# One run of all tiles with engine loops and copied row numbers, in a two-layer mixer and expert kernel

## The chip, the cores and the metric

The kernel runs on one core of a Trainium2 chip. Its time is the device time of one execution in microseconds (us). Five engines work side by side, each through its own list of instructions: TensorE (PE), VectorE (DVE), ScalarE (ACT), GpSimd (POOL) and SyncE (SP, which here only starts transfers). They meet at semaphores. PEld is TensorE's loading of weights, which runs beside its matmuls.

## The reference, cut to what matters

Two images of 128 channels and 64 by 64 positions pass two layers. Each layer has a mixer and then an expert network (eight experts, each token goes to two of them).

```python
x = x + _L0_conv_ref(_ln_c(x), ...)       # layer 0: one gate for each image and channel
t = _to_tokens(x)                          # 2 x 4096 tokens of 128 channels
t = t + _L0_ffn_ref(_ln_t(t), ...)         # softmax over 8 experts, best 2, shares normalised
x = _from_tokens(t, x)
x = x + _L1_conv_ref(_ln_c(x), ...)        # max pools of sizes 1 to 13, two of them blended by a score
t = _to_tokens(x)
t = t + _L1_ffn_ref(_ln_t(t), ...)         # experts with exact gelu, best 2
x = _from_tokens(t, x)
# one expert:  y = gelu(x @ W1 + b1) @ W2 + b2, 128 -> 512 -> 128
```

## The kernel before

**Units and tiles.** A unit is one layer for one image: unit 0 and 1 are layer 0 for image 0 and 1, unit 2 and 3 are layer 1. For each unit the 8192 pairs of token and expert are sorted by expert and cut into 39 tiles of 256 slots. Tiles are counted 0 to 155 through the program; 39, 78 and 117 are the first of units 1, 2 and 3. Step j of a unit is one turn of the loop in `tile_steps`.

**One tile** passes these stages. POOL gathers its rows of tokens with two indirect DMAs of 128 rows (`gather`, L450: `xg<-xn_rows`). PE transposes them (`turn_x`, L697) and ACT copies the result (`copy_x`, L520: `xT`). PE makes the hidden values (`up`, L706), ACT applies gelu (`activate`, L531: `hT`), PE multiplies by the second matrix (`down`, L718), ACT copies (`copy_y`, L541), PE transposes back (`turn_y`, L728), ACT copies (`copy_rows`, L550: `yr`), and POOL scatters the rows with two more indirect DMAs (`scatter`, L459: `y_rows<-yr`). SP loads the weights of the tile's expert (`load_weights`, L351), three tiles ahead. xg, the weights and yr are rings of four buffers (`RING`).

**The order in a step** is fixed in the code: for step t, PE does `turn_x` of tile t+1, `up` of t, `down` of t-1, `turn_y` of t-2; ACT copies in the same order; POOL gathers tile t+4 (`G_AHEAD`) and then scatters tile t-2. An engine takes its list in order, so what waits holds back everything behind it.

**Runs.** `RUNS = [(0,), (1,), (2,), (3,)]`: each unit is a run of its own. It ends with two more steps that empty the pipeline, and the next unit's first gathers follow the last scatter on POOL. All steps are written out; no engine loops.

**Work between the tiles.** `WHEN` lists for each unit at which step (and fraction: after `up`, after `down`) every engine puts in the work for other units. In unit 0 that is the routing of unit 1. In unit 1 it is, for image 0: `outputs` (SP waits for all scatters of unit 0, then loads its results, L368), `combine` on DVE (L1146, which adds the experts' results to the tokens), `mix_state` and `mix_norm` (PE turns tokens to channels, ACT copies), the max pools on DVE (L1177 to L1196), and then the routing of unit 2: `route_turn` (L644 on PE, L503 on ACT), `route_products` (L661), DVE's choice of experts (L1025 on), `route_slots` (L671), four `route_invert` of 16 matmuls (L681), after which DVE has the row numbers (L1112 to L1120). Unit 2 does the same for image 1 and the routing of unit 3. DVE takes this in the order of the program, without regard to steps. In unit 3 only results are combined, and the final turning back of image 0 stands at step 20.

**Row numbers.** DVE writes them for a whole unit into `tile_rows`, and the indirect DMAs read the column of their tile from there.

## Time and profile before

| | |
|---|---|
| median of 3 runs | 1268.28 us (1260.07 to 1268.85) |
| the profiled execution | 1272.95 us |
| its span, first to last instruction | 1271.1 us |
| mean granted TensorE clock | 0.824 of full |
| busy: PE, DVE, ACT, POOL | 923.5, 579.4, 545.1, 706.6 us |
| first gather; first ACT copy of xT of units 0, 1, 2, 3 | 158.4; 165.9, 426.0, 709.3, 990.3 us |
| last ACT copy of a tile's rows; end | 1234.2; 1271.1 us |

Busy shares are averages over stages with different limits; indirect DMAs on POOL count as busy while POOL writes their descriptors. A row of the timeline gives start, length, engine, line, operation, what it writes and reads, the count, and in brackets how long the engine had been idle before it and what it waited for. Ends of matmuls are modelled, so the times at which ACT starts a copy are the surer mark of when PE was done. "remote" in a wait means that the profile has no record of what released it in time.

### The profile page before, as it was taken

What the parts mean: (1) busy time and instruction counts of PE and PEld (TensorE: products, weight loads), DVE (VectorE), ACT (ScalarE), POOL (GpSimd) and SP (SyncE); (2) the same over time, 40 slices, a digit from 0 to 9 for tenths busy, and PEclk for the clock granted to TensorE, in tenths of its full rate; (3) what the DMA queues carried; (4) which work ended last, traced back from release to release, by engine and by line L of the source; (5) the groups of instructions that cost most, each with busy time, mean ns of one, the idle gap of its engine ahead of it and who ended that gap; (6) DMA issues with size and microseconds to landing.
All of it is one profiled execution on the core that took longest, in us unless ns stands there. A gap on an engine that the chain in (4) does not pass through costs nothing.

```text
span 1271.1 us, 14305 instructions
## 1 busy us (share of the span) xinstructions
PE 923.5 (73%) x4116; PEld 740.2 (58%) x4116; DVE 579.4 (46%) x1273; ACT 545.1 (43%) x1363; POOL 706.6 (56%) x650
## 2 busy tenths in 40 slices
PE   5216568899977579765998679776988677778772
PEld 4115256776765468554866567665866556666551
DVE  7977822270300647995470738995460003100006
ACT  6303144462444356443553455443553334545341
POOL 3410065576665657787353657887254567656662
PEclk8555578998998789998888789988788789878895
DMA  3000323353544634433162634443153246435435
GB/s 143 1 0 17 116 87 106 101 160 101 188 137 116 216 114 144 127 122 112 56 164 91 218 118 139 132 129 97 58 165 106 78 149 205 157 100 194 112 83 199
DMA packets 51453, 154.32 MB, mean 121 GB/s; under 512 B 14432, under 2 KB 14453, under 8 KB 50864
## 3 DMA queue, kind: packets, MB, share of 16 engines
q1 hardware_dynamic: 31408, 116.11, 27.0%
q0 software_dynamic: 19968, 37.29, 10.9%
q8 instruction: 35, 0.57, 0.2%
q14 instruction: 42, 0.34, 0.1%
HBM read 123.96 MB, written 33.03 MB: 124 GB/s over the span
## 4 chain that ended last, share of the span: by engine, by line
PE 40%; issue 15%; another core or an unknown queue 12%; POOL 12%; ACT 10%; DVE 6%; DMA 5%; POOLq 0%; ACTq 0%; DVEq 0%; SPq 0%
PE h_ps L706 14%; PE yT_ps L718 11%; POOL y_rows L459 6%; POOL xg L450 6%; PE acc_ps L681 6%; PE turn_ps L644 4%; DMA xg<-xn_rows,tile_rows 4%; ACT hT L531 4%; PE acc_ps L661 2%; PE xT_ps L697 2%; PE yr_ps L728 1%; ACT work L568 1%; ACT yr L550 1%; DVE tok L1146 1%
## 5 line engine op out<-in xcount | busy, mean ns | idle before, releaser
L459 POOL DMA_INDIRECT y_rows<-yr,tile_rows x312 | 337.4, 1081 | 316.4 <-ACT yr L550 230.2
L450 POOL DMA_INDIRECT xg<-xn_rows,tile_rows x312 | 330.9, 1060 | 186.1 <-issue 93.9
L706 PE MATMUL h_ps<-xT,expert 128*128 128x256 f32 x1248 | 354.8, 432 | 57.0 <-ACT hT L531 46.4
L718 PE MATMUL yT_ps<-hT,expert 128*128 128x256 f32 x1248 | 326.8, 409 | 23.3 <-ACT yT L541 14.2
L531 ACT ACTIVATE hT<-h_ps,expert 128x256 f32<-128x256 f32 x624 | 255.3, 477 | 154.2 <-PE h_ps L706 79.9
L706 PEld LDWEIGHTS h_ps<-xT,expert 128*128 128x128 f32 x1248 | 257.2, 218 | 106.5 <-issue 52.2
L718 PEld LDWEIGHTS yT_ps<-hT,expert 128*128 128x128 f32 x1248 | 257.3, 209 | 73.7 <-ACT yT L541 19.4
L1146 DVE SCALAR_TENSOR_TENSOR tok<-work,share,tok 128x128 f32<-128x128 f32 x224 | 66.0, 368 | 379.4 <-DMA work<-y_rows 287.5
L541 ACT ACTIVATE yT<-yT_ps,expert 128x256 f32<-128x256 f32 x156 | 74.3, 476 | 192.1 <-PE yT_ps L718 112.4
L697 PE MATMUL xT_ps<-ident,xg 128*128 128x128 f32 x312 | 69.0, 306 | 113.0 <-DMA xg<-xn_rows,tile_rows 105.7
L520 ACT ACTIVATE xT<-xT_ps 128x256 f32<-128x256 f32 x156 | 60.5, 388 | 188.3 <-PE xT_ps L697 114.9
L697 PEld LDWEIGHTS xT_ps<-ident,xg 128*128 128x128 f32 x312 | 40.6, 155 | 128.7 <-DMA xg<-xn_rows,tile_rows 116.1
L644 PE MATMUL turn_ps<-ident,tok 128*128 128x128 f32 x192 | 38.5, 358 | 52.2 <-DVE tok L1142 25.2
L896 DVE BATCH_NORM_STATS2 stats<-tok 128x6 f32<-128x128 f32 x192 | 39.4, 288 | 78.7 <-ACT tok L503 46.1
L550 ACT ACTIVATE yr<-yr_ps 128x256 f32<-128x256 f32 x156 | 59.5, 382 | 34.1 <-PE yr_ps L728 24.8
L1196 DVE SCALAR_TENSOR_TENSOR state<-work,mix_hot,state 128x1344 f32<-128x1344 f32 (+1 forms) x42 | 66.4, 1637 | 0.5
L644 PEld LDWEIGHTS turn_ps<-ident,tok 128*128 128x128 f32 x192 | 29.6, 184 | 59.7 <-DVE tok L1142 27.0
L728 PE MATMUL yr_ps<-ident,yT 128*128 128x128 f32 x312 | 62.0, 282 | 2.8 <-ACT yr L550 2.8
L728 PEld LDWEIGHTS yr_ps<-ident,yT 128*128 128x128 f32 x312 | 45.3, 147 | 19.8 <-ACT yT L541 3.7
L644 PE MATMUL turn_ps<-ident,state 128*128 128x128 f32 x192 | 34.1, 330 | 26.6 <-ACT tok L503 9.7
L1183 DVE TENSOR_TENSOR work<-work 128x1344 f32<-128x1344 f32 (+1 forms) x36 | 53.1, 1532 | 0.4
L1177 DVE TENSOR_TENSOR work<-work 128x1302 f32<-128x1302 f32 (+1 forms) x36 | 53.1, 1531 | 0.3
(187 smaller groups left out, 730.3 us busy)
## 6 DMA issues: line engine op xcount, KB each, us to landing
expert<-in_experts SPq DMA_DIRECT2D x156, 514.5 KB
work<-y_rows SPq DMA_DIRECT2D x32, 512.0 KB, 6.8
xn_rows<-work SPq DMA_DIRECT2D x16, 512.0 KB, 3.8
xg<-xn_rows,tile_rows POOLq DMA_INDIRECT x312
y_rows<-yr,tile_rows POOLq DMA_INDIRECT x312
state<-in_x SPq DMA_DIRECT2D x4, 1024.0 KB, 8.1
out<-state SPq DMA_DIRECT2D x8, 512.0 KB
shared<-in_first SPq DMA_DIRECT2D x1, 323.5 KB
```

The source lines that it names most:

```text
L450: pool.indirect_dma_start(xg[:, s, h, :], None, xn_rows[unit], bass.IndirectOffsetOnAxis(ap=tile_rows[unit % 2][:, at, 0, h:h + 1], axis=0)) \
L459: pool.indirect_dma_start(y_rows[unit], bass.IndirectOffsetOnAxis(ap=tile_rows[unit % 2][:, at, 1, h:h + 1], axis=0), yr[:, s, h, :], None ...
L531: ins = act.activation(hT[:, s, c, :], h_ps[c // 2][:, c % 2, :], func, bias=expert[:, t.slot(RING), BIAS + c:BIAS + c + 1])
L541: act.activation(yT[:, s, :], yT_ps[:, 0:SLOTS], ACT.Identity, bias=expert[:, t.slot(RING, d), EXPERT - 1:EXPERT]) \
L550: act.activation(yr[:, s, :, :], yr_ps[:, 0:HALVES, :], ACT.Copy).then_inc(s_yr_sb, 1)
L644: mm = pe.transpose(bank[:, k * P:(k + 1) * P], source(t), ident[:])
L681: mm = pe.matmul(acc_ps[:, 0:2 * n], hot_lane[:, :, t], hot_block[:, :, :, t] .rearrange("p a q -> p (a q)"), start=(k == 0 and t == 0), s ...
L697: mm = pe.transpose(xT_ps[:, h * P:(h + 1) * P], xg[:, t.slot(RING, d), h, :], ident[:])
L706: mm = pe.matmul(h_ps[c // 2][:, c % 2, :], expert[:, t.slot(RING), c * P:(c + 1) * P], xT[:, t.slot(2), :], start=True, stop=True)
L718: mm = pe.matmul(yT_ps[:, 0:SLOTS], expert[:, t.slot(RING, d), HIDDEN + c * P:HIDDEN + (c + 1) * P], hT[:, s, c, :], start=(c == 0), stop= ...
L728: mm = pe.transpose(yr_ps[:, h, :], yT[:, s, h * P:(h + 1) * P], ident[:])
L1146: ins = dve.scalar_tensor_tensor(tok[b][:, t, :], work_tok[1 + k][:, t, :], share[b][:, k, t:t + 1], tok[b][:, t, :], ALU.mult, ALU.add)
```

## The change

All units become one run (`RUNS = [(0, 1, 2, 3)]`): no emptying between them, the tile loop of PE, ACT, POOL and SP goes on across a unit's border. Near a border the gathers look ahead by 2 tiles (`BORDER`) instead of 4, worked out by `reach` and `due`. On POOL the scatter of tile t-2 now stands ahead of the gathers of a step.

From step 7 (`PEEL`) on, wherever at least 8 steps follow without work in between, an engine runs them in a loop of 4 tiles (`Fori`) with semaphore values in registers. [...] `tile_rows` becomes float, since ACT converts.

The mixing and routing steps stand at other places: fewer fractions, more in one place.

```diff
-RUNS = [(0,), (1,), (2,), (3,)]
+RUNS = [(0, 1, 2, 3)]
+BORDER = 2
 ...
-    return [(0, "outputs", b, 0, 1, 2, 3), (2, "mix_state", b, 0), (3, "mix_state", b, 1), (4, "mix_state", b, 2),
+    return [(1, "outputs", b, 0, 1, 2, 3), (4, "mix_state", b, 0), (5, "mix_state", b, 1), (6, "mix_state", b, 2),
 ...
+def reach(s, ahead, short):
+    unit, j = divmod(s, TILES)
+    last = (unit + 1) * TILES - 1
+    first = next(r for r in RUNS if unit in r)[0] * TILES
+    end = next(r for r in RUNS if unit in r)[-1] * TILES + TILES - 1
+    if s < first or (j == 0 and s > first):
+        return s + (ahead if s < first else short)
+    return min(end, s + ahead if s + ahead <= last else max(last, s + short))
 ...
 def tile_steps(eng, unit, step, between):
 ...
+    while j < TILES + 2 * ends_run(unit):
+        if j < TILES:
+            insert(j)
+        end = min([int(p) for p in between if p > j] + [TILES - AHEAD])
+        if j >= PEEL and end - j >= 2 * RING:
+            times = (end - j) // RING
+            with eng.Fori(0, times) as i:
+                for k in range(RING):
+                    step(Tile(unit, j + k, i), lambda part: None)
 ...
             def gather(t, d):
-                if t.old(d - RING):
-                    pool.wait_ge(s_xt_ps, t.done(d - RING))
+                pool.wait_ge(s_g_idx, t.done(d))
+                pool.sem_inc(s_begun, 1)
                 for h in range(HALVES):
-                    ...IndirectOffsetOnAxis(ap=tile_rows[unit % 2][:, at, 0, h:h + 1], axis=0))
+                    ...IndirectOffsetOnAxis(ap=g_slot[:, s, h:h + 1], axis=0))
 ...
                 def step(t, mid):
-                    if t.has(G_AHEAD):
-                        gather(t, G_AHEAD)
                     if t.has(-2):
                         scatter(t, -2)
+                    for d in due(t, G_AHEAD, BORDER):
+                        gather(t, d)
 ...
+            def set_gather(t, d):          # on ACT
+                unit, at = t.at(d)
+                act.activation(g_slot[:, t.slot(RING, d), :], tile_rows[unit % 2][:, bass.ds(at, 1), 0, :]
+                               .rearrange("p a h -> p (a h)"), ACT.Copy).then_inc(s_g_idx, 1)
 ...
             def copy_rows(t, d):
+                act.activation(s_slot[:, s, :], tile_rows[unit % 2][:, bass.ds(at, 1), 1, :]
+                               .rearrange("p a h -> p (a h)"), ACT.Copy)
```

The other places are: mixing `mix_state` 4 to 7 (were 2 to 5), `mix_norm` 9.3 in one piece (7.3 to 8.3), `mix_score` 10 and 11 (9 and 10.3), `route_turn` and `route_products` 30 in one piece (27.6 to 28.6), `route_slots` 31 (31.3), `route_invert` 33 and 34 (33.3 to 35.3); in unit 0 `route_turn` 9 (4 and 6), products 10 and 11 (8 and 10), slots 14 (13.3), `route_invert` 20 and 21 (20 to 24).

**POOL at the border from unit 0 to unit 1**, before. L450 is a gather, L459 a scatter, two DMAs for a tile; the first row is the end of unit 0's steps.

```order
L450 DMA xg<-xn_rows,tile_rows 128x128 x2
L459 DMA y_rows<-yr,tile_rows 8192x128 x14
L450 DMA xg<-xn_rows,tile_rows 128x128 x14
L459 DMA y_rows<-yr,tile_rows 8192x128 x2
L450 DMA xg<-xn_rows,tile_rows 128x128 x2
```

The same place with the change (L500 gather, L509 scatter).

```order
L500 DMA xg<-xn_rows,g_slot 128x128 x2
L509 DMA y_rows<-yr,s_slot 8192x128 x6
L500 DMA xg<-xn_rows,g_slot 128x128 x2
L509 DMA y_rows<-yr,s_slot 8192x128 x2
L500 DMA xg<-xn_rows,g_slot 128x128 x2
L509 DMA y_rows<-yr,s_slot 8192x128 x2
L500 DMA xg<-xn_rows,g_slot 128x128 x2
L509 DMA y_rows<-yr,s_slot 8192x128 x2
L500 DMA xg<-xn_rows,g_slot 128x128 x6
L509 DMA y_rows<-yr,s_slot 8192x128 x2
```

Before, all seven last scatters pass and then seven tiles are gathered in a row. Now three scatters (tiles 33, 34, 35) pass and tile 39 is gathered; then scatter 36 and gather 40, scatter 37 and gather 41, scatter 38 and gathers 42, 43 and 44.

**PE at the routing of unit 2**, in unit 1, before, from the first half of `route_turn` (steps 27 to 31).

```order
L644 MATMUL turn_ps<-ident,state 128x128 x16
L697 MATMUL xT_ps<-ident,xg 128x128 x2
L706 MATMUL h_ps<-xT,expert 128x256 x4
L661 MATMUL acc_ps<-routerT,state 128x8 x16
L718 MATMUL yT_ps<-hT,expert 128x256 x4
L661 MATMUL acc_ps<-routerT,state 128x8 x16
L728 MATMUL yr_ps<-ident,yT 128x128 x2
```

The same with the change, from step 30.

```order
L713 MATMUL turn_ps<-ident,state 128x128 x32
L730 MATMUL acc_ps<-routerT,state 128x8 x32
L766 MATMUL xT_ps<-ident,xg 128x128 x2
L775 MATMUL h_ps<-xT,expert 128x256 x4
L787 MATMUL yT_ps<-hT,expert 128x256 x4
L797 MATMUL yr_ps<-ident,yT 128x128 x2
L740 MATMUL turn_ps<-chosen_any,before 128x256
L740 MATMUL turn_ps<-chosen_any,ones 128x256
```

The routing is packed together and begins two to three steps later; the four pieces of 16 inverting matmuls become two of 32.

## Rows read from the trace of the kernel before

**Rows 1.** Who waited for whom: us in total, times, longest.

```profile
POOL y_rows L459 <- ACT yr L550: 230.2, 62, 18.3
...
ACT hT L531 <- remote: 56.9, 32, 4.8
```

**Rows 2.** Windows, copies of xT on ACT alone: us, busy (count), clock, DMA share, GB/s.

```profile
294.20:400.00 105.80, 6.58 (x17) 0.90 0.45 137
...
510.00:586.00 76.00, 4.60 (x12) 0.95 0.41 127
...
1010.00:1105.00 95.00, 5.82 (x16) 0.89 0.51 167
```

**Rows 3.** Windows, POOL alone, while DVE makes the max pools.

```profile
510.50:586.00 75.50, 60.87 (x49) 0.95 0.41 128
```

**Rows 4.** Timeline, ACT in unit 3: two of its stops.

```profile
1004.34 0.84 ACT L531 ACTIVATE hT<-h_ps,expert 128x256 f32<-128x256 f32 x2 [4.75 <-remote]
...
1021.33 0.38 ACT L520 ACTIVATE xT<-xT_ps 128x256 f32<-128x256 f32 x1 [1.70 <-remote]
```

**Rows 5.** The page: the DMA queue that brings instructions, packets, MB, share.

```profile
q8 instruction: 35, 0.57, 0.2%
```

**Rows 6.** Timeline at the border to unit 1: ACT's copies of tiles 38, 39, 42, outputs, PE.

```profile
400.08 0.39 ACT L520 ACTIVATE xT<-xT_ps 128x256 f32<-128x256 f32 x1
...
414.96 0.98 POOL L459 DMA_INDIRECT y_rows<-yr,tile_rows  x1 [0.30 <-issue]
...
417.11 4.35 SPq L368 DMA_DIRECT2D work<-y_rows  x8
...
422.37 4.42 DVE L1146 SCALAR_TENSOR_TENSOR tok<-work,share,tok 128x128 f32<-128x128 f32 x16 [86.10 <-DMA work<-y_rows]
...
425.98 0.38 ACT L520 ACTIVATE xT<-xT_ps 128x256 f32<-128x256 f32 x1 [14.62 <-PE xT_ps L697]
...
427.94 3.62 PE L706 MATMUL h_ps<-xT,expert 128*128 128x256 f32 x8
...
431.77 1.89 PE L706 MATMUL h_ps<-xT,expert 128*128 128x256 f32 x8
...
436.83 0.39 ACT L520 ACTIVATE xT<-xT_ps 128x256 f32<-128x256 f32 x1
```

**Rows 7.** Timeline, ACT: one step at full clock.

```profile
969.57 0.39 ACT L520 ACTIVATE xT<-xT_ps 128x256 f32<-128x256 f32 x1
...
973.20 0.38 ACT L550 ACTIVATE yr<-yr_ps 128x256 f32<-128x256 f32 x1
```

**Rows 8.** Timeline: a copy of rows, its scatters, the next gather, all in unit 3.

```profile
1010.14 0.38 ACT L550 ACTIVATE yr<-yr_ps 128x256 f32<-128x256 f32 x1
...
1011.32 1.02 POOL L459 DMA_INDIRECT y_rows<-yr,tile_rows  x1 [8.34 <-ACT yr L550]
...
1013.95 0.99 POOL L450 DMA_INDIRECT xg<-xn_rows,tile_rows  x1 [0.30 <-issue]
```

**Rows 9.** Timeline: the first gather of unit 3, and ACT's copy of that tile.

```profile
985.74 0.99 POOL L450 DMA_INDIRECT xg<-xn_rows,tile_rows  x1 [0.30 <-issue]
...
990.25 0.38 ACT L520 ACTIVATE xT<-xT_ps 128x256 f32<-128x256 f32 x1 [9.41 <-PE xT_ps L697]
```

**Rows 10.** Timeline in unit 1: max pools begin, routing's turns begin, tile 77's copy.

```profile
482.29 0.16 DVE L1165 TENSOR_REDUCE gap<-gap_parts 128x1 f32<-128x8 f32 x1 [21.82 <-ACT work L510]
...
590.74 1.04 PE L644 MATMUL turn_ps<-ident,state 128*128 128x128 f32 x8
...
684.70 0.39 ACT L520 ACTIVATE xT<-xT_ps 128x256 f32<-128x256 f32 x1
```

**Rows 11.** Windows, the inverting matmuls L681 alone: PE and PEld busy (count).

```profile
590.00:678.30 88.30, 18.33 (x64) 9.42 (x64) 0.80 0.36 99
```

**Rows 12.** Lines, by form: small instructions near those that are added on ACT.

```profile
L531 ACT ACT_TABLE_LOAD x5 | 6.4, 1283 | 1.4 <-issue 1.4
...
L510 ACT ACTIVATION_READ_ACCUMULATOR work<-turn_ps 128x1 f32 x16 | 3.2, 202 | 0.0
```

More of the change, by code:

```diff
@@ L100, with __init__ @@
 class Tile:
-    def __init__(self, unit, j):
-        self.s = unit * TILES + j
+    def __init__(self, unit, j, i=None):
+        self.s, self.i = unit * TILES + j, i
         run = next(r for r in RUNS if unit in r)
         self.first, self.last = run[0] * TILES, (run[-1] + 1) * TILES - 1
+        self.loop_unit, self.loop_at = unit, j
     def at(self, d=0):
+        if self.i is not None:
+            return self.loop_unit, self.i * RING + (self.loop_at + d)
         return divmod(self.s + d, TILES)
     def has(self, d=0):
-        return self.first <= self.s + d <= self.last
+        return self.i is not None or self.first <= self.s + d <= self.last
     def old(self, d):
@@ L116, in done @@
     def done(self, d=0, per=1, part=None):
-        return (self.s + d) * per + (per if part is None else part)
+        n = (self.s + d) * per + (per if part is None else part)
+        return n if self.i is None else self.i * (RING * per) + n
     def slot(self, n, d=0):
@@ L122, in landed, with tile_steps @@
     def landed(self, d=0, each=1):
-        return ((self.s + d) // RING + 1) * 16 * each
-def tile_steps(unit, step, between):
-    extra = 2 * ends_run(unit)
+        n = ((self.s + d) // RING + 1) * 16 * each
+        return n if self.i is None else self.i * (16 * each) + n
+def tile_steps(eng, unit, step, between):
     def insert(at):
@@ L131, in insert, with due @@
             between[round(at, 1)]()
-    for j in range(TILES + extra):
-        insert(j)
-        step(Tile(unit, j), lambda part, j=j: insert(j + part))
-    if extra:
-        insert(TILES + extra)
+    j = 0
+    while j < TILES + 2 * ends_run(unit):
[7 more added lines that the diff above has]
+                    step(Tile(unit, j + k, i), lambda part: None)
+            j += times * RING
+        else:
+            step(Tile(unit, j), lambda part, j=j: insert(j + part))
+            j += 1
+    insert(TILES)
+def reach(s, ahead, short):
[6 more added lines that the diff above has]
+    return min(end, s + ahead if s + ahead <= last else max(last, s + short))
+def due(t, ahead, short):
+    if t.i is not None:
+        return [ahead]
+    if t.s > t.last:
+        return []
+    before = reach(t.s - 1, ahead, short) if t.s > t.first else t.first + ahead - 1
+    return [n - t.s for n in range(before + 1, reach(t.s, ahead, short) + 1)]
 def begins_run(u):
@@ L248, in build @@
         tile_expert = [sb(f"tile_expert{i}", [P, TILES], I32) for i in range(2)]
[L249 removed]
+        tile_rows = [sb(f"tile_rows{i}", [P, TILES, 2, HALVES]) for i in range(2)]
         gap_parts = sb("gap_parts", [P, GROUPS])
@@ L585, in tiles @@
                 if begins_run(u):
+                    act.wait_ge(s_rows, u + 1)
+                    for d in range(G_AHEAD):
+                        set_gather(Tile(u, 0), d)
                     copy_x(Tile(u, 0), 0)
+                    set_gather(Tile(u, 0), G_AHEAD)
                 def step(t, mid):
@@ L590, in step @@
                         copy_x(t, 1)
+                    ahead = due(t, AHEAD, BORDER + 1)
+                    if ahead == [AHEAD]:
+                        set_gather(t, AHEAD)
                     if t.has(0):
@@ L598, in step @@
                         copy_rows(t, -2)
-                tile_steps(u, step, plan(u, route_turn=route_turn, route_exp=route_exp, mix_state=mix_state, mix_norm=mix_norm,
+                    if ahead != [AHEAD]:
+                        for d in ahead:
+                            if t.at(d) == (u + 1, 0):
+                                act.wait_ge(s_rows, u + 2)
+                            set_gather(t, d)
+                tile_steps(act, u, step, plan(u, route_turn=route_turn, route_exp=route_exp, mix_state=mix_state, mix_norm=mix_norm,
                                               route_rows=route_rows, mix_score=mix_score, last_turn=last_turn))
```

58 lines of the change are left out of this document (31 added, 27 removed).

## The prediction, made before the result was known

> **What bounds the kernel now.** I read the page first, then who waited for whom, then windows over single stages, then the timeline at a border. The busy shares (PE 73%, POOL 56%) name no bound, so I went by pace: how often ACT copies an xT, once for each tile.
>
> The waits say that POOL's scatters stood 230.2 us for ACT's copies of rows [rows 1], so POOL is mostly not late. In the windows unit 0's second half makes 17 tiles in 105.8 us, 6.2 us a tile, and unit 3 has 16 copies, 15 intervals, in 95 us, 6.3 us a tile [rows 2]. Two floors lie below. PE's own step at full clock takes 3.63 us from ACT's xT to its yr [rows 7]. POOL's four DMAs take 5.2 us a tile: a pair of scatters 1013.95 - 1011.32 = 2.63 us [rows 8], and a pair of gathers about as much.
>
> While DVE makes the max pools, POOL is the bound: 49 DMAs busy for 60.87 us plus 0.30 us of issue each are 75.6 of 75.5 us [rows 3], and a tile takes 6.3 us [rows 2]. Outside it, something else costs 1 us a tile. ACT's timeline shows it: about 17 us apart, so every third tile, ACT stands on "remote" [rows 4], 56.9 us for hT alone [rows 1], although the gathers and weights of those tiles had landed before. PE must have been late there, with its list as the suspect: 35 packets of instructions, 0.57 MB, came through one queue [rows 5], and that is a third thing that comes at a steady count of PE instructions. I take these stops as the price of the written-out list, with less certainty than the two floors.
>
> **The change, part by part.** The sum is made against the profiled execution, 1272.95 us.
>
> *Borders.* Before, from ACT's copy of the last tile of unit 0 to that of the fourth of unit 1: 436.83 - 400.08 = 36.75 us [rows 6]; the other two borders are alike. What is removed is the emptying and the empty start. What is added is a new chain: POOL gathers tile 39 only after scatter 35, 40 after 36, 41 after 37, 42 after 38. Tile 35's rows are copied at the end of PE's step 37, and tile 39 is the first thing that PE wants in step 38; `up` of tile 38 is queued behind it on PE, and ACT, and so POOL's next scatter, wait behind that. The chain is: yr copy to scatter 1011.32 - 1010.14 = 1.18 us, two scatters 2.63 us [rows 8], first gather to ACT's copy of its tile 990.25 - 985.74 = 4.51 us [rows 9]: 8.32 us in which PE does nothing. Then the step, 3.63 us at full clock [rows 7]. Four such: 4 x 11.95 = 47.8 us. But PE idles for 8 us in each, and after an idle stretch it runs at the low level: behind the border of before, 8 matmul records took 3.62 us against 1.89 us one tile later [rows 6], 1.2 against 2.4 GHz. With the last three steps at that level it is 47.8 + 3 x 3.63 = 58.7 us. I take the middle, 53: +16 us a border, **+48 us** for three; bounds +33 and +66.
>
> *Outputs before weights.* SP waits at step 1 for the last scatter, then issues eight loads of 512 KB, then the weights of the fifth tile. Before, PE was not waiting then. From yr 38: 1.18 + 1.3 + 2.15 (last scatter to outputs, 417.11 - 414.96 [rows 6]) = 4.6 us, then 4.2 MB at the page's best slices, 200 GB/s, 21 us, so 26 us; PE wants these weights 8.3 + 3 x 5 = 23 us after yr 38. **+3 us** a kernel for one partial wait in three; 0 to +12.
>
> *The DVE chain.* Outputs of unit 0 come at about 400 + 12 + 28 + 5 + 5 = 450 instead of 417, so `combine` starts at 455 instead of 422.4 [rows 6], 33 us later. Does unit 2 wait for it? From `combine` to the normalised rows takes 482.29 - 21.82 - 422.37 = 38 us, and then DVE idled 21.8 us for PE and ACT [rows 10]. Now: rows at 493, `mix_norm` in one piece about 12 us, max pools from 506, 590.74 - 482.29 = 108 us long [rows 10], ready at 614. PE comes to step 30 after 20.7 steps of 5.7 us, at 624. So DVE's lateness is just swallowed by its old idle time and PE decides. From there 15.6 us of turns, 8 of products, 18.3 of inverting matmuls [rows 11], 7 steps of about 4.5, 8 us of waiting for the one-hots: 82 us to the copy of tile 77, at 706; before 684.70 [rows 10]. That is +21 us for a unit of which the border is 16 and the weights 1: **+8 us** for units 1 and 2 together beyond what is counted; -10 to +25, since the packed routing may save up to 12 us a unit and a late DVE cost as much.
>
> *Loops.* PE loops over 12 steps in unit 0, 16 each in units 1 and 2, 24 in unit 3. In units 1 and 2 they lie under the max pools, where POOL is the bound [rows 3]: nothing gained. In unit 0 and 3 the pace can fall from 6.2 to POOL's 5.2 plus 0.1 for register and semaphore instructions: 36 steps x 1.0 = -36 us. In unit 0 ACT's loop holds two table loads of 1.28 us [rows 12] in each of four turns, since an exp stands just ahead of it; half of 10 us is on the path: +5. Together **-30 us**; bounds 0 (the stops stay) and -45. The rule of the Trainium skill, Runtime: NRT & Kernel Launch, section Instruction fetch mechanics, speaks against this: fetching a straight list is said to be hidden, and a taken branch that leaves the loaded window to stall. By it, the loops would give nothing and the sum stood at +64; the stops in the trace, with inputs there, disagree with its first half, and of its second half no row shows anything.
>
> *The copies of row numbers* are 312 more instructions on ACT, nearest to the accumulator reads of 0.2 us [rows 12]: 0.4 us a tile on an engine that is 43% busy, beside PE. On the path lies one before the first gather. On POOL two increments and a few register instructions a tile count where it is saturated, some 40 tiles: 0.1 us each, **+5 us** in all; 0 to +12.
>
> *Packing of unit 0's routing:* the same PE work in larger pieces; POOL catches up after each. 0, -8 to +8.
>
> Sum: 48 + 3 + 8 - 30 + 5 = +34 us, 1272.95 + 34 = 1307 us. The median of the runs is 4.7 us below the profiled execution, so **1302 us**.
>
> **The rivals.**
>
> 1. *The loops give nothing back.* Each backward branch or each crossing inside the body (four tiles of PE's list) costs what the stops cost. For: the stops were not tied to a cause by any row. Against: a body that repeats need not be brought again. -30 becomes 0: 1332 us.
> 2. *Even.* PE recovers its clock inside each border step (+33 instead of +48), the weights are in time, the packed routing saves the 8 that I charge: 33 + 0 + 0 - 30 + 0 = +3, about 1270 us. For: the low level lasted one tile at the border shown [rows 6]. Against: here the idle stretch comes back each step.
> 3. *Faster: the stops are the real bound of the routing stretches.* The packed routing takes large matmul groups out of the tile steps; the path from `route_turn` to the last tile, 94 us now (590.74 to 684.70 [rows 10]), falls to its work, 15.6 + 8 + 18.3 + 7 x 3.63 = 67 us, in units 1 and 2, -27 each against my -12: -30 us more. It decides if the routing ends more than 20 us before step 37 wants its rows. Sum +4; with the loops at -45 and the borders at +33 it is -26, 1242 us. For: DVE idled there for PE. Against: DVE's own 13 us of one-hots stand between, and POOL still needs 5.2 us a step.
>
> Chances: my forecast 0.50, rival 1 0.15, even 0.20, faster 0.15. What a measurement here can tell from no change is about 1%, 12.7 us. So slower by over 1% 0.65, within 1% 0.20, faster 0.15. The range leaves out most of the faster case and the far tail of rival 1: 1262 to 1342 us; the forecast's own is 1285 to 1325.
>
> **What the next profile would show.** Right: at each border four intervals of 11 to 15 us between ACT's copies of xT, PE idle about 8 us in each with a gather as the releaser, and a low clock; `combine` of unit 1 some 30 us after the unit's first tile instead of before it; loops in unit 3 at 5.2 to 5.4 us a tile without "remote" waits; the max pool stretch still at 6.3. Wrong: border intervals under 10 us; `route_turn` waiting for DVE by more than 10 us; loop steps at 6 us or more, with instruction packets not much fewer than 35.

## The result, and the profile after

The changed kernel takes 1383.34 us (median; 1377.72 to 1388.62), the kernel before 1267.45 us: a ratio of 1.093, 95% interval 1.086 to 1.100, about 116 us slower. Forecast were 1302 us and a range of 1262 to 1342. The direction was right, the size was not.

The page of the changed kernel, profiled at 1377.72 us, has these lines (busy time and share; the clock by fortieths; the instruction queue; the chain; then groups with busy time, mean and what ended the idle time before them):

```profile
span 1375.9 us, 15949 instructions
...
PE 936.5 (68%) x4116; PEld 750.2 (55%) x4116; DVE 578.5 (42%) x1273; ACT 584.3 (42%) x1682; POOL 701.8 (51%) x650
...
PEclk8555599988888799998777699999878788899885
...
q8 instruction: 27, 0.44, 0.1%
...
PE 36%; issue 18%; DMA 11%; DVE 9%; POOL 9%; another core or an unknown queue 9%; ACT 7%; POOLq 0%; ACTq 0%; DVEq 0%; SPq 0%
...
L509 POOL DMA_INDIRECT y_rows<-yr,s_slot x312 | 336.1, 1077 | 426.8 <-ACT yr L607 341.7
...
L766 PE MATMUL xT_ps<-ident,xg 128*128 128x128 f32 x312 | 72.8, 320 | 245.1 <-DMA xg<-xn_rows,g_slot 221.9
```

The last group's line before:

```profile
L697 PE MATMUL xT_ps<-ident,xg 128*128 128x128 f32 x312 | 69.0, 306 | 113.0 <-DMA xg<-xn_rows,tile_rows 105.7
```

Work hardly grew (ACT by 39 us, its slot copies and table loads). Waiting did: POOL's scatters stood 341.7 us for ACT's copies of rows where they had stood 230.2 [rows 1], and PE stood 221.9 us for gathers where it had stood 105.7. The loops were there: 27 instruction packets in place of 35 [rows 5].

ACT's copies of xT give a clock with one tick a tile. Against before, the changed kernel was behind at tile 38 by 13.0 us, at tile 42 by 33.7, at 77 by 44.1, at 81 by 68.9, at 116 by 73.3, at 120 by 93.3 and at 155 by 100.4; the tail adds 4.4. Nearly two thirds of it (65.5 of 104.8 us) were lost in three times four tiles, 38 to 42, 77 to 81 and 116 to 120. The timeline of the second and third interval of the first border (start, duration, engine, line, operation; idle time and releaser in brackets):

```profile
438.36 0.69 PE L766 MATMUL xT_ps<-ident,xg 128*128 128x128 f32 x2 [7.97 <-DMA xg<-xn_rows,g_slot]
438.84 3.52 PE L775 MATMUL h_ps<-xT,expert 128*128 128x256 f32 x8
...
442.20 1.89 PE L787 MATMUL yT_ps<-hT,expert 128*128 128x256 f32 x8
...
444.59 0.37 ACT L607 ACTIVATE yr<-yr_ps 128x256 f32<-128x256 f32 x1
...
445.85 1.01 POOL L509 DMA_INDIRECT y_rows<-yr,s_slot  x1 [9.02 <-ACT yr L607]
447.16 1.00 POOL L509 DMA_INDIRECT y_rows<-yr,s_slot  x1 [0.30 <-issue]
448.47 0.99 POOL L500 DMA_INDIRECT xg<-xn_rows,g_slot  x1 [0.30 <-issue]
...
452.98 0.38 ACT L574 ACTIVATE xT<-xT_ps 128x256 f32<-128x256 f32 x1 [7.92 <-PE xT_ps L766]
```

From ACT's copy of rows to its next copy of xT are 452.98 - 444.59 = 8.39 us (forecast 8.32), in which PE does nothing. Then comes a step in two halves: the eight matmuls of `up` take 3.52 us, the eight of `down` 1.89 us. The granted clock was 0.50 in the first half and 1.00 in the second, so PE has its full clock back inside each step and goes idle with it. From xT to rows the step takes 5.50 us (439.09 to 444.59), between the 3.63 us of full clock [rows 7] and twice that. The windows of these two halves, and of the whole interval of tile 42 (busy PE, PEld, DVE, ACT, POOL, then the granted clock, DMA share, GB/s):

```profile
438.80:442.10 3.30, 3.30 (x10) 2.68 (x9) 0.00 (x0) 1.22 (x3) 0.00 (x0) 0.50 0.00 0
442.20:444.60 2.40, 2.11 (x11) 1.61 (x9) 0.00 (x0) 1.31 (x5) 0.00 (x0) 1.00 0.00 0
...
453.00:470.50 17.50, 5.77 (x21) 4.62 (x21) 0.92 (x4) 3.15 (x11) 7.75 (x8) 0.70 0.34 106
```

Over the three borders eight of the twelve gaps from rows to the next xT take 8.3 to 8.5 us, and eleven of the twelve steps 5.3 to 6.1 us (the very first 3.54). The last gap of each border is longer, at the first border so:

```profile
462.25 0.99 POOL L500 DMA_INDIRECT xg<-xn_rows,g_slot  x1 [0.30 <-issue]
463.09 4.91 SPq L417 DMA_DIRECT2D work<-y_rows  x8
...
469.81 0.69 PE L766 MATMUL xT_ps<-ident,xg 128*128 128x128 f32 x2 [11.73 <-DMA xg<-xn_rows,g_slot]
...
470.54 0.38 ACT L574 ACTIVATE xT<-xT_ps 128x256 f32<-128x256 f32 x1 [11.52 <-issue]
```

From this gather to ACT's copy of its tile are 8.29 us, where the three gathers before it took 4.5. The eight loads of unit 0's outputs (`work<-y_rows`) start beside it. At the second border, also with outputs, the same stretch is 8.7 us; at the third, where none are loaded, 5.7.

The DVE chain of unit 1: combine, the pools' begin, their last piece, the routing's turns:

```profile
469.58 17.39 DVE L1215 SCALAR_TENSOR_TENSOR tok<-work,share,tok 128x128 f32<-128x128 f32 x64 [145.14 <-DMA work<-y_rows]
...
524.08 0.16 DVE L1234 TENSOR_REDUCE gap<-gap_parts 128x1 f32<-128x8 f32 x1 [18.22 <-ACT work L558]
...
621.83 4.74 DVE L1265 SCALAR_TENSOR_TENSOR state<-work,mix_hot,state 128x1344 f32<-128x1344 f32 x3
...
645.12 1.04 PE L713 MATMUL turn_ps<-ident,state 128*128 128x128 f32 x8
```

ACT's copy of tile 77 follows at 728.8. DVE's result is there at 626.6, and the turns stand ahead of PE's step 30, at 645.1: 18.5 us unused. Before, DVE's last piece began at 581.02, and the turns ran at 590.74 [rows 10], 5 us after its end.

The stops that the prediction hoped to be rid of are still there inside the loops. ACT in unit 3:

```profile
1194.87 1.57 ACT L585 ACTIVATE hT<-h_ps,expert 128x256 f32<-128x256 f32 x4 [5.96 <-remote]
...
1273.04 0.84 ACT L585 ACTIVATE hT<-h_ps,expert 128x256 f32<-128x256 f32 x2 [4.45 <-remote]
```

Windows over 35 copies of xT in unit 3, before and then changed, give 214.9 and 219.5 us, 6.1 and 6.3 us a tile:

```profile
1010.30:1225.20 214.90, 13.33 (x35) 0.87 0.48 152
```
```profile
1106.10:1325.60 219.50, 13.40 (x35) 0.89 0.47 149
```

### The profile page after: what moved, and what is told of

Read it like the earlier page. It is cut to its first block, busy times and chain, and to the rows that moved or that the text cites. A ratio compares the mean times of both kernels' runs of the same rounds, so it can differ in the third digit from the quotient of the medians.

```text
span 1375.9 us, 15949 instructions
## 1 busy us (share of the span) xinstructions
PE 936.5 (68%) x4116; PEld 750.2 (55%) x4116; DVE 578.5 (42%) x1273; ACT 584.3 (42%) x1682; POOL 701.8 (51%) x650
## 4 chain that ended last, share of the span: by engine, by line
PE 36%; issue 18%; DMA 11%; DVE 9%; POOL 9%; another core or an unknown queue 9%; ACT 7%; POOLq 0%; ACTq 0%; DVEq 0%; SPq 0%
PE h_ps L775 13%; DMA xg<-xn_rows,g_slot 10%; PE yT_ps L787 8%; PE acc_ps L750 5%; POOL xg L500 5%; POOL y_rows L509 4%; PE turn_ps L713 4%; PE acc_ps L730 3%; ACT hT L585 3%; PE xT_ps L766 2%; ACT yr L607 1%; DVE tok L1215 1%; ACT yT L595 1%; DVE stats L965 1%
## 5 line engine op out<-in xcount | busy, mean ns | idle before, releaser
L509 POOL DMA_INDIRECT y_rows<-yr,s_slot x312 | 336.1, 1077 | 426.8 <-ACT yr L607 341.7
L500 POOL DMA_INDIRECT xg<-xn_rows,g_slot x312 | 327.0, 1048 | 185.5 <-issue 92.3
L775 PE MATMUL h_ps<-xT,expert 128*128 128x256 f32 x1248 | 374.7, 453 | 26.5 <-ACT hT L585 21.4
L787 PE MATMUL yT_ps<-hT,expert 128*128 128x256 f32 x1248 | 315.0, 398 | 10.5 <-ACT yT L595 7.6
L775 PEld LDWEIGHTS h_ps<-xT,expert 128*128 128x128 f32 x1248 | 272.9, 230 | 75.6 <-ACT hT L585 25.5
L787 PEld LDWEIGHTS yT_ps<-hT,expert 128*128 128x128 f32 x1248 | 253.8, 204 | 57.4 <-ACT yT L595 11.9
L766 PE MATMUL xT_ps<-ident,xg 128*128 128x128 f32 x312 | 72.8, 320 | 245.1 <-DMA xg<-xn_rows,g_slot 221.9
L713 PE MATMUL turn_ps<-ident,tok 128*128 128x128 f32 x192 | 34.9, 336 | 48.9 <-DVE tok L1211 25.3
L750 PE MATMUL acc_ps<-hot_blocks,shared 128*128 128x156 bf16 x128 | 36.6, 455 | 24.3 <-DVE hot_blocks L1162 21.8
```

The source lines that it names most:

```text
L500: pool.indirect_dma_start(xg[:, s, h, :], None, xn_rows[t.at(d)[0]], bass.IndirectOffsetOnAxis(ap=g_slot[:, s, h:h + 1], axis=0)) \
L509: pool.indirect_dma_start(y_rows[t.at(d)[0]], bass.IndirectOffsetOnAxis(ap=s_slot[:, s, h:h + 1], axis=0), yr[:, s, h, :], None, bounds_ch ...
L713: mm = pe.transpose(bank[:, k * P:(k + 1) * P], source(t), ident[:])
L750: mm = pe.matmul(acc_ps[:, 0:2 * n], hot_lane[:, :, t], hot_block[:, :, :, t] .rearrange("p a q -> p (a q)"), start=(k == 0 and t == 0), s ...
L766: mm = pe.transpose(xT_ps[:, h * P:(h + 1) * P], xg[:, t.slot(RING, d), h, :], ident[:])
L775: mm = pe.matmul(h_ps[c // 2][:, c % 2, :], expert[:, t.slot(RING), c * P:(c + 1) * P], xT[:, t.slot(2), :], start=True, stop=True)
```

## The experiments

All ratios are to the kernel before on the same chip, with 95% intervals; 1% is 12.7 us. The runs without a diff of new code differ from their neighbour by the constants shown.

### From the kernel before to the changed one, a part at a time

**Slot copies alone.** These are ACT's copies of each tile's two row numbers, without loops, borders or changed places. The edit is shown against the next run below: gathers again ahead of scatters.

```
+                    for d in due(t, G_AHEAD, BORDER):
+                        gather(t, d)
                     if t.has(-2):
                         scatter(t, -2)
-                    for d in due(t, G_AHEAD, BORDER):
...
-                        gather(t, d)
```

> The run with slot copies and order (ratio 1.0155), now with the gather ahead of the scatter as before: the copies and increments are left. If they are the cost, 1.01 to 1.02; if the order is, 0.998 to 1.006.

Measured 1.0055 [1.0011, 1.0098]: the copies and increments cost about 7 us, where 5 were priced.

**Slot copies and scatter first.** The changed kernel with loops off, single runs and the WHEN table of before (the table is left out here):

```
-PEEL = 7
+PEEL = 200
-RUNS = [(0, 1, 2, 3)]
+RUNS = [(0,), (1,), (2,), (3,)]
```

> Loops, borders and places all as before; what is left of the change is the two copies of row numbers a tile on ACT, the two increments on POOL and the scatters issued ahead of the gathers. By the prediction 5 us over the kernel before: about 1273 us. Rival: with scatter(t-2) ahead of gather(t+4) each gather starts up to one pair of scatters (2.6 us) later, and where PE stands for it that is paid: 1285 to 1300 us.

Measured 1.0155 [1.0069, 1.0241]. So the order costs some 1% more, a term that the prediction did not have; the intervals of the two runs overlap, and it is likely, not shown. One thing in its trace will matter below: all of ACT's waits on "remote" together are 106.7 us in 48 times, where the kernel before has 191.8 us in 93, and yet this kernel is not faster.

**With the loops.** The same, with them:

```
-PEEL = 200
+PEEL = 7
```

> Borders and places as before, loops, slot copies and scatter first as changed. Against the run with slot copies and the order alone (ratio 1.0155) it shows the loops alone. Prediction: 25 us faster, ratio 0.996. Theory of the count: in the loops a tile has 50 PE instructions instead of 44, so 5 to 12 us slower, ratio 1.02 to 1.025.

Measured 1.0234 [1.0161, 1.0307], 10 us over the run without loops, within the noise of the two. The gain of 25 us is excluded.

**With the changed places.** The changed kernel with single runs:

```
-RUNS = [(0, 1, 2, 3)]
+RUNS = [(0,), (1,), (2,), (3,)]
```

> The changed kernel with each unit as a run of its own (emptied and started anew, as before), loops and places as changed. The term of the borders alone: by the prediction 48 + 3 us less than the changed kernel, about 1332 us. By the intervals between ACT's xT copies in the two traces (from tile 38 to the eighth tile of the next unit +22.6, +26.4, +23.2 us) 72 us less: 1311 us.

Measured 1.0473 [1.0406, 1.0541]. The changed places add 2.4%, 30 us; and from here to the whole change (1.0927) the borders add 4.5%, 57 us, between the two expectations.

The path sums to 7 + 13 + 10 + 30 + 57 = 117 us.

### From the other end

**No loops.** The changed kernel with:

```
-PEEL = 7
+PEEL = 200
```

> The changed kernel with its loops written out; all else as it is. Theory of the prediction (PE stops for its list of instructions, loops spare that): 20 to 30 us slower than the changed kernel, about 1405 us. Rival (PE stops after about 130 instructions that it executes, looped or not, as both traces look): the loops spare nothing and cost their register instructions and the table loads of unit 0, so 5 to 20 us faster than the changed kernel, about 1370 us.

Measured 1.0975 [1.0909, 1.1041] beside 1.0927 [1.0855, 1.0998]: no difference that can be told. The 20 to 30 us of the prediction's theory are not there, and the rival's gain is not seen either. The page shows 35 instruction packets again, so the 27 of the changed kernel were the loops' doing.

**Old places.** The changed kernel with the WHEN table of before (unit 3's last entries at 39):

```
-    return [(1, "outputs", b, 0, 1, 2, 3), (4, "mix_state", b, 0), (5, "mix_state", b, 1), (6, "mix_state", b, 2),
+    return [(0, "outputs", b, 0, 1, 2, 3), (2, "mix_state", b, 0), (3, "mix_state", b, 1), (4, "mix_state", b, 2),
...
-    [(9, "route_turn", 1, 0), (9, "route_turn", 1, 1), (10, "route_products", 1, 0), (11, "route_products", 1, 1),
+    [(4, "route_turn", 1, 0), (6, "route_turn", 1, 1), (8, "route_products", 1, 0), (10, "route_products", 1, 1),
```

> The changed kernel with the mixer's and routing's steps where they stood before (outputs at step 0 of the next unit), one run and loops kept. By the prediction places cost 8 us: about 1375 us. Rival: at the changed places unit 0 loses 13 us (routing pieces of 8 and 16 groups in one place, one interval of 15.8 us) and the packed routing of units 1 and 2 costs 14.9 and 11.4 us at one tile but gets 16 back at another: about 1365 us.

Measured 1.0785 [1.0717, 1.0853]: 18 us less. The rival was nearer in the total, and tile 38 came 9.6 us earlier than in the changed kernel, where it had 13. But with single runs the same places cost 30 us. The two differ because in the one run the old places have a price of their own: the mixer's first turns stand at step 2, and PE stands there, ahead of tile 42, for DVE's `combine`:

```profile
467.66 2.16 PE L713 MATMUL turn_ps<-ident,tok 128*128 128x128 f32 x8 [15.86 <-DVE tok L1215]
```

The four intervals at the first border take 66.9 us here and 57.5 in the changed kernel. So the price of the borders and that of the places are not independent; the sum above holds for its own order.

**Gather first at the border.** On the changed kernel (`ahead` holds what `due` gives):

```
+                    early = ahead[:1] if ahead[:1] == [BORDER] else []
+                    for d in early:
...
+                        gather(t, d)
                     if t.has(-2):
                         scatter(t, -2)
-                    for d in due(t, G_AHEAD, BORDER):
...
+                    for d in ahead[len(early):]:
                         gather(t, d)
```

> The changed kernel with one thing turned round: in the steps around a unit's border POOL issues the next gather ahead of the scatter of that step. If the border's price is the chain in the prediction (copy of rows, pair of scatters, gather, copy of xT: 8.3 us in which PE does nothing, and then the step), the chain now runs over two steps, the intervals fall from 12 to 18.7 us to 6 to 9, and the kernel gains 45 to 70 us on the changed one: a ratio to the kernel before of about 1.05. Rival (the short look-ahead itself, the weights and the four MB of outputs set the intervals): less than 15 us gained, ratio above 1.08.

Measured 1.0446 [1.0359, 1.0532]: 4.8%, 61 us, given back by turning a pair of gathers and a pair of scatters round in four steps a border. Its timeline around tile 40:

```profile
416.91 0.97 POOL L500 DMA_INDIRECT xg<-xn_rows,g_slot  x1 [0.30 <-issue]
418.18 1.02 POOL L509 DMA_INDIRECT y_rows<-yr,s_slot  x1 [0.30 <-issue]
419.50 1.00 POOL L509 DMA_INDIRECT y_rows<-yr,s_slot  x1 [0.30 <-issue]
420.81 0.99 POOL L500 DMA_INDIRECT xg<-xn_rows,g_slot  x1 [0.30 <-issue]
421.30 0.38 ACT L578 ACTIVATE xT<-xT_ps 128x256 f32<-128x256 f32 x1 [5.22 <-PE xT_ps L770]
426.74 0.38 ACT L578 ACTIVATE xT<-xT_ps 128x256 f32<-128x256 f32 x1
```

The gather of tile 40 goes out at 420.81, before ACT has copied tile 39, and tile 40 follows it after 5.4 us instead of 14.2. Four intervals now take 30.7 us, less than the 36.75 of before [rows 6]. So the order is most of the border's loss. What is left sits behind it: at the two borders with outputs the next four tiles take 37.6 and 36.5 us (before 20.9 and 21.4), at the third 25.5 (before 22.9). There the gather of tile 43 (446.08) stands beside the output loads (446.92) and takes 9.3 us to ACT's copy. That the outputs slow it is the likely reading, and was not tested by itself.

### The places

**Places alone.** The kernel before with the changed WHEN, of which:

```
-            (27.6, "route_turn", u, 0), (28, "route_turn", u, 1), (28.3, "route_products", u, 0),
+            (30, "route_turn", u, 0), (30, "route_turn", u, 1), (30, "route_products", u, 0),
```

> The kernel before with the changed places of the mixer's and routing's steps alone (outputs at step 1, where no border is crossed). By the prediction's own terms 0 to 8 us, ratio up to 1.006. By the two runs with loops and single units (1.0473 with the changed places, 1.0234 with the old) 20 to 35 us slower, ratio 1.016 to 1.028, of it 9 to 10 us between the copies of tiles 67 and 77, and of 106 and 116, where the routing stands packed.

Measured 1.0253 [1.0186, 1.0320], 32 us, with none of the other parts. In its trace 6.5 us are lost up to tile 38; tiles 67 to 77 take 107.2 us (before 98.6) and 106 to 116 107.3 (before 100.0), near what was expected. At the packed routing of unit 1 its timeline has one interval of 37.7 us, where the first three of before were 21.8, 13.4 and 8.1 us:

```profile
605.57 0.38 ACT L520 ACTIVATE xT<-xT_ps 128x256 f32<-128x256 f32 x1 [2.48 <-issue]
609.04 1.04 PE L644 MATMUL turn_ps<-ident,state 128*128 128x128 f32 x8
...
622.86 0.60 ACT L503 ACTIVATE tok<-turn_ps 128x512 f32<-128x512 f32 x1 [5.07 <-remote]
...
629.04 13.66 PE L661 MATMUL acc_ps<-routerT,state 128*128 128x8 f32 x64
...
643.26 0.38 ACT L520 ACTIVATE xT<-xT_ps 128x256 f32<-128x256 f32 x1 [13.38 <-PE xT_ps L697]
```

**Routing places of units 2 and 3 alone.** The kernel before, with the entries from 27.6 to 35.3 replaced by those at 30 to 34; the last of them:

```
-            (33.3, "route_invert", u, 0, 0), (34, "route_invert", u, 0, 1), (34.6, "route_invert", u, 1, 0),
+            (33, "route_invert", u, 0, 0), (33, "route_invert", u, 0, 1), (34, "route_invert", u, 1, 0),
```

> The kernel before with only the routing steps of units 2 and 3 where the change puts them (turns and products packed ahead of step 30, inversions ahead of 33 and 34). The prediction took the packing as a gain of up to 12 us a unit or a cost of as much. From the two runs with loops: tile 67 to 77 and 106 to 116 cost 9 to 10 us more each, so ratio 1.014 to 1.016. Rival (what the packing loses at one tile it gives back at the next): 1.000 to 1.005.

Measured 1.0122 [1.0043, 1.0202]. In its trace tiles 67 to 77 take 102.8 us (before 98.6) and 106 to 116 101.6 (before 100.0), less than the ratio says; more than half of the 15 us has no place in this one execution.

**Mixer places alone.** The kernel before, with:

```
-    return [(0, "outputs", b, 0, 1, 2, 3), (2, "mix_state", b, 0), (3, "mix_state", b, 1), (4, "mix_state", b, 2),
+    return [(1, "outputs", b, 0, 1, 2, 3), (4, "mix_state", b, 0), (5, "mix_state", b, 1), (6, "mix_state", b, 2),
...
```

> The kernel before with only the mixer's steps (and outputs at step 1) of units 1 and 2 where the change puts them. From the run with all changed places (1.0253) less 1.015 for the routing, unit 0 and the mixer share 1 per cent: 1.003 to 1.008. Rival: with outputs and products later DVE's chain to the next routing moves on by 5 us and more a unit: 1.01 or above.

Measured 1.0016 [0.9973, 1.0058]: nothing. With routing 1.2 and mixer 0.2, 1.1% of the places remain, some 14 us. They are not unit 0 alone, where turns, products and inversions are packed and begin up to five steps later: the traces show 6.5 to 9.6 us for it. The packed routings cost 8.6 + 7.3 us with the mixer late as well, and 4.2 + 1.6 us without, so the parts don't simply add up. Neither unit 0 nor the pair was run by itself.

### What the stops are not

**Sixteen more waits a tile on PE**, in the kernel before. The trace has 1312 more instructions, 8.4 a tile (two waits share one), not the 2496 of the expectation.

```
+                    for _ in range(16):
+                        pe.wait_ge(s_const, IDENT)
```

> The kernel before with 16 more waits a tile on PE, each for a semaphore that has its value since the start: no work, 2496 more instructions (8963 before). Theory of the count (a stop about every 130 instructions that PE executes): the stops in the routing stretches now come every 2.1 tiles instead of every 2.9, and the kernel is 50 to 110 us slower, a part of which is the waits' own 0.8 us a tile. Rival (stops at a fixed time or number of tiles, or for a transfer): they stay 2.9 tiles, 17 to 19 us apart, and the kernel is 0 to 50 us slower.

Measured 1.0140 [1.0071, 1.0208], 18 us. Its page has 40 instruction packets: 8963 + 1312 = 10275 PE instructions are 40.1 x 256, as 8963 are 35.0 x 256, so the queue does carry PE's list. The 50 to 110 us of the theory of the count did not come. The distances of the stops are weaker evidence. In the traces of unit 3, from one first late copy to the next, the first four are 132, 141, 115, 140 PE instructions before and 156, 152, 160, 155 here; in matmuls and weight loads alone 120, 128, 104, 128 before and 120, 120, 120, 120 here, as if only these counted. But the next ones are 300, 128, 128, 140 and 160 before, and 88, 220, 116, 168, 112 and 100 here. And if a stop is a stretch in which ACT starts 3 us or more behind the record of its matmul, unit 3 has 10 of them before, 12 here, and 12 in the run with mixer places alone, whose PE list has as many instructions as before. So no steady count is shown, of either kind; what falls is the price.

**Fewer waits**, in the kernel before: those that an earlier wait of PE already covers.

```
+                if not t.has(1):
                     pe.wait_ge(s_xt_sb, t.done())
...
+                    if c % 2 == 0 and not t.has(d + 1):
                         pe.wait_ge(s_h_sb, t.done(d, 2, c // 2 + 1))
```

> The kernel before without PE's waits that an earlier wait of PE already holds (for xT in up, for hT in down). Each tile has one or two PE instructions fewer. Theory of the count: 150 to 310 instructions fewer are 1 to 2.4 stops of 5 to 6 us fewer, of which about 6 in 10 lie outside the max pool stretches: 3 to 9 us faster, ratio 0.993 to 0.998. Rival (the count has nothing to do with it): no change, 0.999 to 1.001.

Measured 1.0007 [0.9963, 1.0051]: no change; the interval excludes the larger half of what the theory expected, not all of it.

**Less matrix work**, in the kernel before:

```
+                    if c % 2:
+                        continue
                     mm = pe.matmul(yT_ps[:, 0:SLOTS], ...
-                                   start=(c == 0), stop=(c == CHUNKS - 1))
+                                   start=(c == 0), stop=(c == CHUNKS - 2))
```

> The kernel before with two of the four products of each tile's down left out (chunks 1 and 3 of the hidden values don't enter the result): 32 weight loads and matmuls a tile instead of 40. If PE's stops come with its matrix work, they stay about 120 such instructions apart, now every 3.75 tiles, or are gone where POOL's 5.2 us sets the pace, and tiles in the last unit take 5.2 to 5.5 us: 40 us or more faster, ratio 0.95 to 0.97. Rival (stops at a fixed time or number of tiles, from transfers or the like): every 2.9 tiles still, 6 us a tile, less than 15 us faster.

Measured 0.9703 [0.9609, 0.9798], 38 us where the theory asked for 40 or more. The first five distances came as it said, 108, 120, 112, 96 and 104 matmuls and weight loads, now about every 3.4 tiles. But the pace did not: tiles in unit 3 took 6.04 us (before 6.20), not 5.2 to 5.5. The stops were no smaller: all of ACT's waits on "remote" are 198.7 us in 98 times (191.8 in 93 before), and the row of hT (total, times, longest), 56.9 before [rows 1], is here as below. The mean granted clock fell to 0.77, so this run changes more than one thing.

```profile
ACT hT L531 <- remote: 76.1, 33, 6.1
```

**Half the weights' traffic**, in the kernel before:

```
+                part = slice(0, EXPERT) if t.s + d < RING else slice(HIDDEN, EXPERT)
-                sp.dma_start(expert[:, s, :], experts[layer, bass.ds(e, 1)].rearrange("a p n -> (a p) n")) \
+                sp.dma_start(expert[:, s, part], experts[layer, bass.ds(e, 1)].rearrange("a p n -> (a p) n")[:, part]) \
```

> The kernel before with only the second half of each tile's expert loaded from the fifth tile on (the first half in the buffers is that of other experts): 257 KB a tile instead of 514. If PE's stops come from the transfers (a full memory port, weights late), they shrink or go: 20 us or more faster. If they come with PE's own work: the same time within 8 us and the stops still about 120 weight loads and matmuls apart.

Measured 0.9976 [0.9931, 1.0022], the first stops 116, 96, 128, 104 and 112 matmuls and weight loads apart. So the traffic of the weights doesn't make them.

### A try for a better kernel

From the kernel before: one run, gather first in the border steps, outputs at step 2, mixer three steps later.

```
-RUNS = [(0,), (1,), (2,), (3,)]
+RUNS = [(0, 1, 2, 3)]
+BORDER = 2
...
-    return [(0, "outputs", b, 0, 1, 2, 3), (2, "mix_state", b, 0), (3, "mix_state", b, 1), (4, "mix_state", b, 2),
+    return [(2, "outputs", b, 0, 1, 2, 3), (5, "mix_state", b, 0), (6, "mix_state", b, 1), (7, "mix_state", b, 2),
...
+                    for d in ahead[:1]:
...
+                        gather(t, d)
                     if t.has(-2):
                         scatter(t, -2)
```

> A try for a better kernel, from the kernel before: one run of all units, the next gather ahead of the scatter in the steps around a border, outputs loaded from step 2 and the mixer's steps 3 later; no loops, no slot copies, routing where it was. With the gather first the changed kernel's four border intervals took 30.6 us where before took 36.75. If that holds and DVE's later start is swallowed (it stood idle 21.8 us for route_turn), 5 to 25 us faster than before, ratio 0.98 to 0.996. Rival: the four MB of outputs in one piece hold up the weights of the sixth tile (they follow on the same queue) and the mixer comes later: no change or up to 15 us slower.

Measured 1.0046 [1.0012, 1.0081]. The border did become faster: tile 39 came 22.0 us and tile 42 12.8 us earlier than before (of which 4.7 were there at tile 38). Tile 67 was 4.4 us earlier, tile 70 1.5 us later. Two things took the gain:

```profile
426.27 1.00 POOL L479 DMA_INDIRECT y_rows<-yr,tile_rows  x1 [0.30 <-issue]
...
427.57 0.99 POOL L470 DMA_INDIRECT xg<-xn_rows,tile_rows  x1 [0.30 <-issue]
...
428.39 3.98 SPq L388 DMA_DIRECT2D work<-y_rows  x8
...
433.46 15.07 SPq L371 DMA_DIRECT2D expert<-in_experts  x3
433.83 4.46 DVE L1169 SCALAR_TENSOR_TENSOR tok<-work,share,tok 128x128 f32<-128x128 f32 x16 [103.67 <-DMA work<-y_rows]
...
436.85 0.69 PE L720 MATMUL xT_ps<-ident,xg 128*128 128x128 f32 x2 [9.38 <-DMA xg<-xn_rows,tile_rows]
```

The first is tile 43. Its gather (427.57) goes out beside the outputs, PE stands 9.38 us for it, and the tile is 4.0 us earlier than before, less than the 4.7 of tile 38: what the border gave was gone there. At the second border PE stands 8.0 us at this place, at the third, without outputs, 4.5. The second is DVE's chain.

The old unit's last scatter goes out among the new unit's work, at 426.27 instead of 414.96 [rows 6], and DVE begins its chain to the next routing, 168 us long before (422.37 to 590.74 [rows 6, 10]), 11.5 us later. The routing's turns run at 597.4, 6.7 us later than before, and the 5 us that PE took after DVE's end are gone: here the chain decides. DVE's share of the chain that ended last rose from 6% to 20%. Emptying the pipeline brings the outputs early, and that is a part of what its 36.75 us buy. It isn't the whole account: in unit 3, with neither outputs at its start nor a routing to come, 8.2 us were gained at the border and 3 were left at the last tile.

**The outputs in quarters**, on that kernel:

```
-    return [(2, "outputs", b, 0, 1, 2, 3), (5, "mix_state", b, 0), (6, "mix_state", b, 1), (7, "mix_state", b, 2),
+    return [(2, "outputs", b, 0), (3, "outputs", b, 1), (4, "outputs", b, 2), (5, "outputs", b, 3), (5, "mix_state", b, 0), (6, "mix_state", b, 1), (7, "mix_state", b, 2),
```

> The same, with the outputs' four quarters loaded at steps 2, 3, 4 and 5, between the weights of the tiles, not in one piece. If the outputs ahead of the weights cost something (12.7 us at the fifth tile in the gather-first run), 5 to 10 us less than the run before this one; if not, the same.

Measured 1.0029 [0.9981, 1.0078]: the same, so spreading the outputs does not give the time back. Of the kernels here that leave nothing out, none is measurably faster than the one before.

## Why the prediction was wrong, step by step

- **What bounds the kernel.** The two floors held. The third thing, the stops of rows 4, was given a wrong cause, "with its list as the suspect", and a price of 1 us a tile that no run bears out. Three counts that seemed to agree (35 packets, 8963 instructions, stops about every third tile) were no proof: at 44 instructions a tile, 132 instructions and 120 matmuls and weight loads are the same three tiles. And with slot copies and scatter first ACT's "remote" waits nearly halved (191.8 to 106.7 us) with no gain: in unit 3 the 35 tiles from 120 to 155 took 220.9 us there and 218.9 before. What the trace of before could have shown and the prediction did not ask: in the 76 us of max pools from 510 us, with the same list for 12 tiles, the waits have no "remote" on ACT at all. As long a window of unit 3, from 1010 us, has (total, times, longest):

```profile
ACT hT L531 <- remote: 9.6, 4, 3.3
ACT yT L541 <- remote: 9.0, 4, 3.5
ACT xT L520 <- remote: 5.2, 3, 2.1
```

  A price that the list asks would be asked in both.
- **Loops, -30: the step that failed most.** Measured +10 in one comparison and -6 in the other, so 0 within the noise: 30 to 40 of the 81 us missed. The bound 0 and the first rival said so. The rule of the Trainium skill, Runtime: NRT & Kernel Launch, section Instruction fetch mechanics, that fetching a straight list is mostly hidden, was set aside for the rows; the runs with and without loops agree with it (1.0927 and 1.0975, 1.0234 and 1.0155). That a taken branch that leaves the loaded window stalls, its other half, no run shows: with four tiles in a body, loops cost nothing that can be told. The two table loads an iteration did come (16 on ACT in the changed kernel, 9 before), and are within that noise.
- **Places: the second failure, +30 where +8 stood.** The prediction priced the late combine and took the packing as a gain in the routing. From the turns to tile 77 it was: 728.8 - 645.1 = 83.7 us, forecast 82, before 94. The loss lies ahead of it. The prediction let PE reach step 30 at 624 us, ten after DVE; PE came at 645.1, 18.5 us after DVE. A smaller misreading is in there too: the 108 us for the max pools (482.29 to 590.74) hold the 5 us that PE took after DVE's end. And of unit 0, "the same PE work in larger pieces ... 0", the traces show 6.5 to 9.6 us, with one interval of 15.8 us for two packed turns. The rest is not placed; routing and mixer moved together cost more than each alone.
- **Borders, +48: mechanism right, size short.** The chain measured 8.39 us against 8.32, and "I take the middle, 53" was right for a step: 5.3 to 6.1 us, half of it at each level. But the three borders took 57.5, 62.3 and 56.7 us for four tiles against 36.6 to 37.5 before, sum +66 us. They come near the bound of 58.7 us by another way than the bound's, which had whole steps at the low level: at the second and third border the first step was half low too, and the last gap was 9.6 to 12.6 us instead of 8.3. The runs say 57 us for the borders, weights and outputs included.
- **Outputs before weights, +3: priced at the wrong place.** The sum looked at the weights of the fifth tile. What the traces show is a late gather: the last gap of the borders with outputs is 12.2 and 12.6 us, of the one without 9.6. The next four tiles took 4.8, 4.4 and 2.7 us more than before, the last again without outputs. By this comparison outputs cost 2.6 + 3.0 + 2.1 + 1.7 = 9.4 us, within the bound of 12. They are counted in the 57.
- **Copies and POOL, +5:** 7 for the copies. Scatter before gather in every step, by the two runs some 13 us, likely and not shown, had no term. It was told in the change and left unpriced: every gather goes out one pair of scatters, 2.6 us, later.
- **The rivals.** The first (1332 us) had the right mechanism with the wrong border and places. Faster was wrong. Of even's condition, that PE recovers its clock inside each border step, half came: it recovered in the middle of each, and the idle gap that followed cost it again. "The low level lasted one tile" [rows 6] was the wrong row to lean on, since there PE had all its inputs at hand.

So the sum +34 becomes +117 by 57 - 51 = 6, places 22, loops 40, order 13 and copies 2: 83 us more, all on one side. The 6 flatter the border term: in the trace the borders' twelve intervals grew by 66 us, and with the old places the borders cost 70 (1.0785 - 1.0234), not 57. The range let each term move, but not together.

## What to carry to other kernels

Where a queue carries both the results of old work and the inputs of new work, put the inputs first in the steps where the look-ahead is short: that one order was worth 61 us here. Where a gather has no slack, look too at what large transfers start beside it: 4.5 us from gather to use became 8 to 10 beside eight loads of 512 KB. Before overlapping two stages, ask who waits for the last result of the first; if a long chain on another engine starts from it, emptying quickly may be worth as much as keeping the engine busy. And a stall that recurs at a steady count needs a second stretch in which the suspected count runs on and the other candidates don't, before it is given a cause; and a run in which it becomes rarer, before it is given a price.

## What was not expected

PE's stops. Their cause stays open, and so does what they cost. They come where PE is let run at its own pace, mostly some 96 to 160 matmuls and weight loads apart (16 to 27 us), now and then 220 to 300. They hold ACT's copies 2 to 12 us after the matmuls' own records, and mostly a low stretch of the granted clock follows. They did not go away with 15% more instructions, with a looped list, with half the weights' traffic or with a fifth of the matrix work gone. With slot copies and scatters first they became rarer (5 in unit 3's last 35 tiles, by the 3 us mark, where before has 10; 11 again with the loops), and the time stayed. While POOL holds a tile to 6.3 us [rows 2, 3], ACT has no wait on "remote" in the 76 us looked at, and the pace outside comes out the same 6.1 to 6.3 us. Whether the recording of instructions itself holds PE up can't be seen in runs that are all recorded; the Trainium skill, NOTIFIC — the notification-queue block, section 7.1, says that the block's inner buffers can hold back the engines that feed it, and no run here shows whether they do.
